# Seven of eight output blocks stored by GpSimd as indirect row writes in place of one SyncE transfer each

## What is computed

```python
# layer 1: layer norms, a decaying complex convolution over time, a SiLU MLP of width 512
h  = layernorm(layernorm(x))*gamma + beta
x1 = spiral_conv(h) + layernorm(x)
x  = x + silu(layernorm(x1) @ w1 + b1) @ w2 + b2 + x1
# layer 2: top-2 of 8 experts, all 8 computed for every token
t       = layernorm(x)
combine = softmax(top2(t @ router.T))          # (tokens, 8), zero but for two
hmid    = gelu(einsum('th,efh->etf', t, ew1) + eb1)
y       = einsum('etf,ehf->eth', hmid, ew2) + eb2
out     = x + einsum('eth,te->th', y, combine)
```

## Time and profile before

| | |
|---|---|
| device time, two runs | 656.67 and 658.28 us, median 657.47 us |
| span of the profiled execution (first to last instruction) | 654.0 us |
| what the median has beside that span | 3.5 us |
| TensorE busy | 552.9 us, 85% |
| VectorE busy | 553.7 us, 85% |
| ScalarE busy | 430.9 us, 66% |
| GpSimd busy | 314.2 us, 48% |
| expert stage, 388 to 440 us (one block, 52 us) | TensorE 49.8, VectorE 46.6, ScalarE 39.8, GpSimd 20.0 us |
| moved by DMA | 45.3 MB, all on one hardware queue but for instructions |

### The profile page before, as it was taken

The page is one execution under the profiler, slowest core; times in us unless marked ns, Lnnn a source line. Parts: engine busy times, 40 slices in busy tenths (PEclk is TensorE's granted clock), DMA queues, the critical chain, the costliest instruction groups (busy, mean ns, idle before and its releaser), DMA issues.

```text
span 654.0 us, 9016 instructions
## 1 busy us (share of the span) xinstructions
PE 552.9 (85%) x2768; PEld 448.8 (69%) x2768; DVE 553.7 (85%) x1048; ACT 430.9 (66%) x540; POOL 314.2 (48%) x252
## 2 busy tenths in 40 slices
PE   1112878988879999899989989989989989999995
PEld 1002667767768887677768868868868868877783
DVE  6989789988778458998898989899898898699796
ACT  2313466645656697696688678778778769767772
POOL 7668967687767102442532441532344244224332
PEclk9999989988989999999999999999999999999998
DMA  7410000000000034051052035016017016006111
GB/s 227 136 57 1 2 0 2 0 0 0 1 1 2 0 95 165 1 200 61 1 173 120 1 96 195 0 36 255 0 32 260 0 33 246 15 1 221 70 33 32
DMA packets 27669, 45.26 MB, mean 69 GB/s; under 512 B 1714, under 2 KB 18610, under 8 KB 27508
## 3 DMA queue, kind: packets, MB, share of 16 engines
q1 hardware_dynamic: 27636, 44.86, 19.9%
HBM read 40.40 MB, written 4.46 MB: 69 GB/s over the span
## 4 chain that ended last, share of the span: by engine, by line
PE 40%; DVE 22%; POOL 16%; issue 13%; ACT 6%; DMA 1%; DVEq 0%; POOLq 0%; ACTq 0%
PE down_p L703 6%; PE down_p L705 6%; PE down_p L704 6%; PE up_p L703 6%; PE up_p L705 5%; DVE hid_lo L1235 5%; PE up_p L704 5%; DVE work L1247 4%; DVE scored L1193 4%; POOL norm_pow L429 3%; POOL resid L461 3%; ACT work L648 3%; POOL work L450 2%; PE down_p L728 2%; POOL scale L442 2%
## 5 line engine op out<-in xcount | busy, mean ns | idle before, releaser
L501 POOL TENSOR_TENSOR work<-work 128x1024 f32<-128x1024 f32 x55 | 138.0, 2508 | 267.5 <-DVE work L1247 267.5
L1235 DVE TENSOR_TENSOR hid_lo<-work,hid_hi 128x1024 fp32r<-128x1024 f32 x128 | 198.5, 1551 | 42.9 <-ACT hid_hi L654 42.1
L648 ACT ACTIVATE work<-up_p,par 128x1024 f32<-128x1024 f32 x128 | 141.5, 1105 | 54.8 <-PE up_p L705 54.8
L654 ACT ACTIVATE hid_hi<-work 128x1024 fp32r<-128x1024 f32 x128 | 135.7, 1060 | 4.3
L703 PE MATMUL down_p<-hid_lo,mw_hi 128*128 128x512 f32 x256 | 104.2, 407 | 5.2 <-DVE hid_lo L1235 4.4
L703 PE MATMUL up_p<-xm_lo,mw_hi 128*128 128x512 f32 x256 | 101.9, 398 | 7.1 <-ACT work L648 7.1
L697 PE MATMUL turn_p<-ident,work 128*128 128x128 f32 x312 | 47.4, 302 | 65.2 <-DVE work L1002 38.8
L705 PE MATMUL down_p<-hid_hi,mw_lo 128*128 128x512 f32 x256 | 101.2, 395 | 0.0
L704 PE MATMUL down_p<-hid_hi,mw_hi 128*128 128x512 f32 x256 | 100.8, 394 | 0.0
L705 PE MATMUL up_p<-xm_hi,mw_lo 128*128 128x512 f32 x256 | 100.7, 393 | 0.0
L704 PE MATMUL up_p<-xm_hi,mw_hi 128*128 128x512 f32 x256 | 100.2, 392 | 0.0
(11 more groups left out here) (159 smaller groups left out, 800.8 us busy)
## 6 DMA issues: line engine op xcount, KB each, us to landing
work<-comb_weights SPq DMA_DIRECT2D x64, 512.0 KB, 6.6
resid<-in_x SPq DMA_DIRECT2D x8, 512.0 KB, 3.8
out<-work SPq DMA_DIRECT2D x7, 512.0 KB, 3.2
work<-in_mw SPq DMA_DIRECT2D x1, 1024.0 KB, 6.7
out<-work SPq DMA_DIRECT2D x2, 256.0 KB, 2.4
work<-in_w SPq DMA_DIRECT2D x1, 256.0 KB
w_sb<-in_w SPq DMA_DIRECT2D x1, 256.0 KB
comb_weights<-work SPq DMA_DIRECT2D x8, 32.0 KB
```

The lines of the kernel that those rows point to most:

```text
L501: g.tensor_tensor(total[q], total[q], part[e % 2], ALU.add).then_inc(s_add, 1)
L648: s.activation(hid[c][e % 2], up_p[c][:, :], ACT.Gelu, bias=par[:, k:k + 1]).then_inc(s_gelu, 1)
L654: s.activation(hid_hi[c][e % 2][:, :], hid[c][e % 2], ACT.Copy).then_inc(done, 1)
L1235: d.tensor_tensor(hid_lo[c][e % 2][:, :], hid[c][e % 2], hid_hi[c][e % 2][:, :].bitcast(f32), ALU.subtract).then_inc(s_elo, 1)
```

## The change

The whole-block stores of blocks 0 to 6 leave SP. GpSimd writes each as eight indirect DMAs: number j takes `result[:, j, :]` (128 partitions of 128 floats, 64 KB) and writes partition p to the output row that `row_of[p, 8n + j]` names, which is 128 (8n + j) + p. The eight are issued in block n+1 right after add 5 (`Step.finish` is 5), and each adds 16 to a new semaphore `s_rows`. The table `row_of` is made by one iota at the start of GpSimd's program, which the next instruction waits for. SP's wait ahead of `weight[0]` and VectorE's wait ahead of the last `finish` are now for `s_rows`. The last block's two half stores stay on SP. The loops of SP and GpSimd over the blocks are written out.

```diff
+        row_of = sb("row_of", [128, TILES - TPB], mybir.dt.uint32)
+        out_rows = out.rearrange("b t d -> (b t) d")
...
-            def store(n):
-                sp.wait_ge(s_out, n + 1)
-                sp.dma_start(out_dram[bass.ds(n, 1), :, :, :].rearrange("a p j d -> (a p) j d"), result)\
-                    .then_inc(s_store, 16)
-
...
-                        after(sp, s_store, (b - 1) * 16)
+                        after(sp, s_rows, (b - 1) * (16 * TPB))
...
-            with sp.Fori(1, LAST) as n:
-                store(n - 1)
+            for n in range(1, LAST):
                 spread(n + 1)
-            store(LAST - 1)
...
-            sp.wait_ge(s_store, 16 * (BATCHES + 1))
+            sp.wait_ge(s_rows, 16 * TPB * LAST)
+            sp.wait_ge(s_store, 16 * 2)
...
+            link(g.iota(row_of[:, :], [[TILE, TILES - TPB]], base=0, channel_multiplier=1))
             link(g.memset(ident[:, :], 0.0))
...
+            def store(n):
+                pool.wait_ge(s_out, n + 1)
+                for j in range(TPB):
+                    k = n * TPB + j
+                    g.indirect_dma_start(out_rows, bass.IndirectOffsetOnAxis(row_of[:, k:k + 1], 0),
+                                         result[:, j, :], None).then_inc(s_rows, 16)
+
             def experts(n, q, more):
...
                     if e == 3 and more:
                         x2_scales(n + 2, n * 2 + (base + 4))
+                    if e == Step.finish and n > 0:
+                        store(n - 1)
...
-            v.wait_ge(s_store, LAST * 16)
+            v.wait_ge(s_rows, LAST * (16 * TPB))
```

More of the change, by code:

```diff
@@ L191, in block_moe_kernel @@
         s_store = sem("block_stored")
+        s_rows = sem("rows_stored")
         s_pc = sem("pool_const_order")
@@ L503, in experts @@
                         x2_scales(n + 2, n * 2 + (base + 4))
+                    if e == Step.finish and n > 0:
+                        store(n - 1)
             x2_scales(0, base)
             x2_scales(1, base + 2)
[L506 to L510, removed]
+            for n in range(LAST - 1):
+                experts(n, n % 2, True)
             experts(LAST - 1, 0, False)
```

## The result

The changed kernel takes 718.98 us (median of two runs, 718.55 and 719.42) where the kernel before takes 657.47 us. The ratio is 1.095, with a 95% interval of 1.089 to 1.100: 61.5 us or 9.5% slower. Forecast were 692.3 us and a range of 668 to 728 us. The profiled execution has a span of 716.0 us, 62.0 more than before.

What follows compares the result with a forecast made beforehand. TensorE was taken as full, DMA bandwidth not the limit. Six gates at 3.4 us late plus 1.6 us clock, plus 4.8 us tail, made 34.8 us: 657.5 to 692.3 us, 5.3% slower, range 668 to 728 us.

Steps and rivals of the forecast that it cites:

- The case that was given 0.60: The forecast itself: an indirect DMA takes GpSimd 0.88 to 1.4 us, weight gates late by 1.6 to 5.8 us.
- the collisions: Rival, chance 0.07: GpSimd's stores held some 0.8 us by each of three `hid_lo`, 2.4 us more per gate and tail; 709 us.
- the slow GpSimd: Rival, chance 0.17: an indirect DMA takes GpSimd x = 1.65 us, gates 7.8 us late, 723 us.
- The bound and the place: Expert stage: TensorE full; `weight[0]` has 7.5 us of slack to its VectorE reader, which has 0.16 us to TensorE.
- The price of one indirect DMA: GpSimd's time for one store, called x: 1.1 us, between powers at 0.57 and 1.65, so 8.8 us per block.
- The sign that was to speak for it: In the new profile, VectorE's operations getting longer beside the stores would show the prediction wrong; no size given.
- d: Lateness of the reader of `weight[0]` at each of six gates: 8x - 5.4 = 3.4 us, x being one indirect DMA's GpSimd time.
- a tail: Last block: block 6's stores delay add 6, and VectorE's last add waits for it, late by 8x - 4.0 = 4.8 us.
- The estimate x = 1.0: GpSimd's time per indirect DMA, estimated from the Trainium skill's about 1 us to first byte; would give 2.6 us late gates.
- the void rival: Rival that `hid_lo` holds up GpSimd's stores (709 us, chance 0.07); by the Trainium skill's inference it would be void.
- The clock term: TensorE behind each of six gates: idling drops its clock from 2.4 to 1.2 GHz for eight matmuls, 1.6 us per gate.
- "No cost at any x": GpSimd's adds 6 and 7, behind the stores, end 7 us before their first VectorE waiter, whatever an indirect DMA takes: 0.

Runs made afterwards that it cites:

- gate_on_vector: Changed kernel with SP's wait for the row stores ahead of `weight[0]` moved to VectorE ahead of each finish, VectorE's block loop written out; 672.7 us, ratio 1.024.
- before_gate_held: Kernel before, SP's own stores, but SP's load of `weight[0]` for blocks 2 to 7 also waits for add 7 of the block before; 686.7 us, ratio 1.043.
- dose_6: Changed kernel with six indirect DMAs per block on GpSimd, the other two tiles stored by SP, both gating `weight[0]`; 697.8 us, ratio 1.061.
- dose_4: Changed kernel with four indirect DMAs per block on GpSimd, the other four tiles stored by SP, both gating `weight[0]`; 669.7 us, ratio 1.019.
- gate_on_vector_last_sp: Changed kernel with the row-store wait moved from SP to VectorE ahead of each finish, and block 6 stored by one SP DMA; 665.1 us, ratio 1.012.
- the control: Kernel before, all stores by SP, with the wait for them moved to VectorE ahead of finish and block loops written out; 655.3 us, ratio 0.996.

## Why the prediction was right, and where its size was off

*Direction, place and range.* The direction and the chain of waits came true. The case that was given 0.60 did not, as it was stated: it had the gates late by 1.6 to 5.8 us, and they are 7.0 us late. 719 us lies between the 709 of the collisions and the 723 of the slow GpSimd, two rivals; the range held it because it was drawn past x = 1.65.

*The bound and the place.* Right. The reader of `weight[0]` was on the path without slack, and 7.5 us was all that the gate had. `gate_on_vector` took the gate away and 46 us with it; `before_gate_held` made it late without a store and lost 30 us.

*The price of one indirect DMA* is the step that was mis-sized. It stood at 1.1 us, the middle between two powers; it is 1.26 alone (0.96 and a gap of 0.30), and 1.60 as it stands in the block, since four of the eight start beside a `hid_lo`. So 12.8 us stand where 8.8 were forecast. The rival of collisions was not an alternative but a second part of the price: 2.4 us per block were put on it, and 12.8 - 8 x 1.26 = 2.7 us were measured. The sign that was to speak for it, longer VectorE operations, did not show: the `hid_lo` beside the stores take 1.22 and 1.23 us, and it is the stores that get longer. With 12.8 the formulas of the prediction give d = 12.8 - 5.4 = 7.4, a tail of 11.3 - 4.0 = 7.3 (there the stores take 11.3 us, for VectorE soon has nothing to do) and 6 x (7.4 + 1.6) + 7.3 = 61.3 us. Measured are 61.5. That this fits so closely is in part luck: the gates are 7.0 us late and not 7.4, since the weight load goes out 1.3 us behind the last store and not 1.9, and what follows each gate costs 2.1 and not 1.6.

*The estimate x = 1.0 and the void rival.* The estimate was too small (1.26 were measured), and the void rival was not void. The Trainium skill (SBUF — State Buffer, Who interferes with whom) infers that descriptor writing passes beside a tensor_tensor. The plain DMAs agree with that, 0.54 us at the median and 0.83 at most, though some start beside `hid_lo`. An indirect one also takes its indices from `row_of` in SBUF, and the same section of the Trainium skill says that two-input VectorE operations collide with GpSimd's reads. The stretch at the start of a store fits that, but no run here reads the indices apart.

*The clock term.* Right in kind, a little small: TensorE idles 6.8 us, comes back at 0.50 and each gate costs 9.1, where the lateness alone is 7.0. That leaves 2.1 for the 1.6 that was charged. `dose_6` has it; `dose_4` is without it at four of the five gates counted. At the lateness forecast it was not certain: of the six gates of `before_gate_held`, late by about as much, one kept the clock at 1.00.

*What VectorE saves.* The `hid_lo` at the end of the block went from 3.27 to 1.22 us, as said, and it turned into waiting: VectorE's 9.02 are 7 of lateness and 2 of that.

*"No cost at any x" for adds 6 and 7.* True for this kernel and only while the gate is late. With the gate gone, 8 us are left that come with the late adds (`gate_on_vector_last_sp`), and spreading the stores took more than half of that back.

*SP, the iota and the loops.* Nothing, as said; the control bounds it at 0.4%.

## What to carry to other kernels

A store is not off the path when a later load waits for it to land: look at what a change of issuer does to the time at which the transfer ends, and compare that with the slack of the gate. Here the weight load goes out 14.2 us behind the end of add 5, where it went out together with that end, and the slack was 7.5 us. Price an issue by what the engine in question does in it: on GpSimd one plain DMA of 1024 rows cost 0.94 us and eight indirect ones of 128 rows 12.8, and all of it stood ahead of the adds queued behind. Where one wait covers another, as the late weights covered the late adds, taking the first away gives back less than its length.

## What was not expected of the hardware

- A plain DMA from GpSimd took 0.94 us for 1024 rows and 0.54 us for 128; an indirect one of 128 rows took 0.96 us plus a gap of 0.30 us before the next, so in these runs the number of issues weighs more than the number of rows.
- VectorE's two-input `hid_lo`, 1.21 us when free, took 4.96 us when it started among eight back-to-back plain DMAs with an add behind them, and 4.01 when it started in an indirect store with an add right behind. It took 1.23 when it started in an indirect store with another store, and so a gap, behind. Why the operation that comes later gets ahead of it stays open.
- TensorE's granted clock fell behind idle times of 6.6 to 7.2 us at all six gates of the changed kernel and behind idle times of 2.6 to 3.8 us at five gates of `before_gate_held`. At the other gate of that run TensorE idled 2.84 us and the clock stayed at 1.00, as it did behind 0.59 us in `dose_4` (VectorE's wait of 1.77 us). So the length of the idle time does not settle it alone in these runs.
